# State-space scans of a Mamba block: the inputs dt\*u\*B of five of sixteen states made by TensorE instead of VectorE

## The reference

```python
u, z = jnp.split(xz, 2, axis=-1)             # 256 channels each
u = silu(causal_conv(u) + convb)
dtr, Bm, Cm = jnp.split(u @ Wx.T, [8, 24], axis=-1)   # 16 states
dt = jax.nn.softplus(dtr @ Wdt.T + bdt)
def step(h, ins):                            # over 512 tokens
    dt_t, u_t, B_t, C_t = ins
    h = jnp.exp(dt_t[..., None] * A) * h + (dt_t * u_t)[..., None] * B_t[:, None, :]
    y_t = jnp.einsum('bdn,bn->bd', h, C_t)
    return (h, y_t)
y = (y + u * Dp) * silu(z)                   # then @ Wout.T
```

## Time and profile before

| | us |
|---|---|
| median of three runs | 1843.81 (1840.83 to 1847.52) |
| the profiled execution | 1826.05 |
| span of its instructions | 1824.2 |
| state-space phase in it | about 0 to 1050 |
| mean granted TensorE clock | 0.822 of full |

### The profile page before, as it was taken

The page is one execution under the profiler, slowest core; times in us unless marked ns, Lnnn a source line. Parts: engine busy times, 40 slices in busy tenths (PEclk is TensorE's granted clock), DMA queues, the critical chain, the costliest instruction groups (busy, mean ns, idle before and its releaser), DMA issues. The chain is left out here.

```text
span 1824.2 us, 27919 instructions
## 1 busy us (share of the span) xinstructions
PE 1289.2 (71%) x8048; PEld 890.3 (49%) x8048; DVE 1453.3 (80%) x2426; ACT 953.1 (52%) x1520; POOL 991.7 (54%) x908
## 2 busy tenths in 40 slices
PE   3666767577567667665776627789889898989743
PEld 1444545355445444453554403345666666656643
DVE  1999999999999999999999716577668686767412
ACT  4556646664665466556655122555555555546411
POOL 1677767776777677777777542014244243432443
PEclk9877877787789678877876557989989898999876
DMA  4122302320221122022202021125365454645762
GB/s 144 41 95 94 117 0 93 116 84 9 116 93 76 41 93 116 4 89 116 93 17 93 0 59 52 56 84 172 121 180 176 140 160 137 194 126 169 213 213 58
DMA packets 114407, 184.87 MB, mean 101 GB/s; under 512 B 10385, under 2 KB 87185, under 8 KB 109969
## 3 DMA queue, kind: packets, MB, share of 16 engines
q1 hardware_dynamic: 110192, 175.15, 28.1%
q0 software_dynamic: 4096, 8.40, 1.7%
HBM read 153.03 MB, written 25.89 MB: 98 GB/s over the span
## 5 line engine op out<-in xcount | busy, mean ns | idle before, releaser
L731 POOL TENSOR_TENSOR hc<-hb,cb 128x512 f32<-128x512 f32 x512 | 653.8, 1295 | 249.4 <-DVE hb L610 213.8
L610 DVE TENSOR_TENSOR_SCAN hb<-da,dbu 128x512 f32<-128x512 f32 x512 | 599.4, 1201 | 5.6 <-DVE stats L635 4.0
L499 ACT ACTIVATE da<-dt,a_neg 128x512 f32<-128x512 f32 x512 | 351.9, 717 | 354.6 <-DVE hb L610 303.3
L331 PE MATMUL yp<-ident,hc 128*128 128x128 f32 x2048 | 356.9, 317 | 65.7 <-POOL hc L731 65.4
L331 PEld LDWEIGHTS yp<-ident,hc 128*128 128x128 f32 x2048 | 296.9, 165 | 174.3 <-POOL hc L731 93.6
L603 DVE TENSOR_TENSOR dbu<-dtu,bp 128x512 f32<-128x512 f32 x512 | 323.6, 676 | 3.4 <-PE bp L319 2.5
L1750 DVE TENSOR_REDUCE mx<-ms 128x1 f32<-128x384 f32 (+3 forms) x352 | 219.2, 638 | 128.4 <-PE ms L1333 126.8
L1623 ACT ACTIVATE pt<-scores,lift 128x512 f32<-128x512 f32 x320 | 216.4, 684 | 180.8 <-PE scores L1374 180.2
L319 PE MATMUL bp<-st,sel 96*128 96x512 bf16 x256 | 116.4, 455 | 155.9 <-DVE dbu L603 153.4
L2084 POOL DMA_INDIRECT xs_scratch<-h2n,posi x64 | 63.5, 992 | 164.6 <-issue 115.0
L285 PE MATMUL wp<-xpad,wu 128*128 128x512 f32 x256 | 136.7, 627 | 22.1 <-ACT xpad L429 15.6
(11 more groups left out here) (215 smaller groups left out, 2077.8 us busy)
## 6 DMA issues: line engine op xcount, KB each, us to landing
cb<-c_scratch SPq DMA_DIRECT2D x16, 3072.0 KB, 12.0
wt<-ffn_w_e SPq DMA_DIRECT2D x120, 384.0 KB, 4.2
cb<-c_scratch SPq DMA_DIRECT2D x16, 1024.0 KB, 4.6
q<-q_scratch SPq DMA_DIRECT2D x96, 96.0 KB
xg<-xs_scratch SPq DMA_DIRECT2D x24, 256.0 KB, 4.2
ys_scratch<-ysb SPq DMA_DIRECT2D x24, 256.0 KB, 2.3
q_scratch<-qp SPq DMA_DIRECT2D x24, 128.0 KB
k<-k_scratch SPq DMA_DIRECT2D x32, 72.0 KB
```

Of the source, the lines that this page charges most:

```text
L331: last = nc.tensor.matmul(yp[:, c, h * P:(h + 1) * P], src[:, c * P:(c + 1) * P], ident[:, :], is_transpose=True, start=(s < 0 and h == 0 ...
L499: nc.scalar.activation(da[:, s % NDA, :], dt[:, d, h, :], ACT.Exp, scale=a_neg[:, d, h, n:n + 1]).then_inc(da_done, 1)
L610: nc.vector.tensor_tensor_scan(hb[:, s % NHB, :], da[:, s % NDA, :], dbu[:, s % 2, :], 0.0, ALU.mult, ALU.add).then_inc(scan_done, 1)
L731: nc.gpsimd.tensor_tensor(hc[:, s % NHC, :], hb[:, s % NHB, :], cb[:, d, s // 2, :], ALU.mult).then_inc(hc_done, 1)
```

## The change

Five states, n = 6, 8, 10, 12 and 14, get their input dt\*u\*B from TensorE, in each of the 16 units. TensorE transposes `dtu` (time on partitions, `pe_dtt`, step 3), and ScalarE copies it to SBUF (`dtt`). B with time on partitions comes from small matmuls (`pe_bt`, step 22, for the next unit) and a copy (`bt`). For each such state, ScalarE makes four 128x128 diagonal matrices, the identity scaled by a column of `bt` (`act_diag`), and TensorE multiplies the transposed `dtu` by them (`pe_fill`): 4 f32 matmuls for each half. The first half goes to `bp[n % 2]` at step 2n - 1 in the place of the selection matmul, the second to a bank of `dbu` at step 2n + 2. VectorE's scans read these banks directly. The products of the state behind such a state no longer stand together before its scans: one follows the first scan of the TensorE-made state, the other its second scan. `dt` and `dtu` have one buffer now instead of two.

```diff
+BY_PE = (6, 8, 10, 12, 14)
+def dbu_banks():
+    banks = [0]
+    for n in range(1, NS):
+        banks.append(1 - banks[-1] if made_by_pe(n - 1) else banks[-1])
+    return banks
+def dbu_bank(d, n):
+    return DBU_BANK[n] ^ (d * N_PE % 2)
...
+        def pe_bt(pe, b, d):
+            pe.wait_ge(silu_done, count(silu_done, b, 4 * d + 4))
+            for c in range(TC):
+                for h in range(NH2):
+                    last = nc.tensor.matmul(wp[:, 1 - d, c * NS:(c + 1) * NS], u[:, h, c * P:(c + 1) * P],
+                                            wx[:, d, h, 0:NS], start=(h == 0), stop=(h == 1))
+            last.then_inc(bt_ready, 1)
...
+        def pe_dtt(pe, b, d):
+            pe.wait_ge(dt_done, count(dt_done, b, 2 * d + 2))
+            pe.wait_ge(soft_done, count(soft_done, b, 8 * d + 8))
+            for g in range(2):
+                for c in (2 * g, 2 * g + 1):
+                    for h in range(NH2):
+                        at = (c % 2) * DI + h * P
+                        last = nc.tensor.transpose(wp[:, g, at:at + P], dtu[:, h, c * P:(c + 1) * P], ident[:, :])
+                last.then_inc(dtt_ready, 1)
...
+        def pe_fill(pe, b, d, n, h):
+            e = BY_PE.index(n)
+            if h == 0:
+                pe.wait_ge(diag_done, count(diag_done, b, TC * (N_PE * d + e + 1)))
+                pe.wait_ge(dtt_done, count(dtt_done, b, 2 * d + 2))
+                pe_bank_free(pe, b, d, n)
+            else:
+                pe.wait_ge(scan_done, count(scan_done, b, STEPS * d + 2 * n - 1))
+            dst = dbu[:, dbu_bank(d, n), :] if h else bp[:, n % 2, :]
+            for c in range(TC):
+                last = nc.tensor.matmul(dst[:, c * P:(c + 1) * P], dtt[:, c, h * P:(h + 1) * P], diag[:, e % 2, c, :],
+                                        start=True, stop=True)
+            last.then_inc(fill_done if h else b_ready, 1)
...
@@ pe_dt
             if h == 0:
+                pe.wait_ge(bt_done, count(bt_done, b, d + 1))
...
@@ pe_unit
                 if s % 2 == 1 and s // 2 + 1 < NS:
-                    pe_b(pe, b, d, s // 2 + 1)
+                    if made_by_pe(s // 2 + 1):
+                        pe_fill(pe, b, d, s // 2 + 1, 0)
+                    else:
+                        pe_b(pe, b, d, s // 2 + 1)
+                if s % 2 == 0 and made_by_pe(s // 2 - 1):
+                    pe_fill(pe, b, d, s // 2 - 1, 1)
...
+                if s == 3:
+                    pe_dtt(pe, b, d)
...
+                    if s == 22:
+                        pe_bt(pe, *front)
...
+        def act_diag(act, b, d, e):
+            act.wait_ge(bt_done, count(bt_done, b, d + 1))
+            act.wait_ge(fill_done, count(fill_done, b, N_PE * d + e - 1))
+            for c in range(TC):
+                nc.scalar.activation(diag[:, e % 2, c, :], ident[:, :], ACT.Copy,
+                                     scale=bt[:, d, c, BY_PE[e]:BY_PE[e] + 1]).then_inc(diag_done, 1)
...
@@ act_front
+            if at == 27:
+                act_bt(act, b, d)
@@ act_unit
                 act_da(act, b, d, s)
+                if s in (8, 9):
+                    act_dtt(act, b, d, s - 8)
+                for e in range(N_PE):
+                    if s == 2 * BY_PE[e] - 1:
+                        act_diag(act, b, d, e)
                 if tail and s in (14, 15):
                     act_ygt(act, *tail, s - 14)
...
@@ dve_dbu
             dve.wait_ge(scan_done, count(scan_done, b, STEPS * d + s - 1))
-            nc.vector.tensor_tensor(dbu[:, s % 2, :], dtu[:, d, h, :], bp[:, n % 2, :],
+            nc.vector.tensor_tensor(dbu[:, dbu_bank(d, n) ^ h, :], dtu[:, h, :], bp[:, n % 2, :],
                                     ALU.mult).then_inc(dbu_done, 1)
...
@@ dve_scan
+            n, h = s // 2, s % 2
+            src = dbu[:, dbu_bank(d, n) ^ h, :]
+            if not made_by_pe(n):
+                dve.wait_ge(dbu_done, count(dbu_done, b, N_DBU * d + made_by_dve(s + 1)))
+            elif h == 0:
+                src = bp[:, n % 2, :]
+                dve.wait_ge(b_ready, count(b_ready, b, NS * d + n + 1))
+            else:
+                src = dbu[:, dbu_bank(d, n), :]
+                dve.wait_ge(fill_done, count(fill_done, b, N_PE * d + BY_PE.index(n) + 1))
...
@@ dve_unit
                 dve_scan(dve, b, d, s)
-                if s % 2 == 1 and s + 1 < STEPS:
-                    dve_dbu(dve, b, d, s + 1)
-                    dve_dbu(dve, b, d, s + 2)
+                n, h = s // 2 + 1, s % 2
+                if n < NS and not made_by_pe(n):
+                    if made_by_pe(n - 1):
+                        dve_dbu(dve, b, d, 2 * n + h)
+                    elif h:
+                        dve_dbu(dve, b, d, 2 * n)
+                        dve_dbu(dve, b, d, 2 * n + 1)
```

More of the change, by code:

```diff
@@ L75, in is_first, with made_by_pe, made_by_dve @@
     return isinstance(b, int) and b == 0
+BY_PE = (6, 8, 10, 12, 14)
+N_PE = len(BY_PE)
+def made_by_pe(n):
+    return n in BY_PE
+def made_by_dve(s):
+    return sum(1 for i in range(s) if not made_by_pe(i // NH2))
+N_DBU = made_by_dve(STEPS)
+def dbu_banks():
[3 more added lines that the diff above has]
+    return banks
+DBU_BANK = dbu_banks()
+def dbu_bank(d, n):
+    return DBU_BANK[n] ^ (d * N_PE % 2)
 def mamba_phase(nc, sems, x, x1, cscr, w):
@@ L131, in mamba_phase @@
         t_relu = sb("t_relu", [P, NH2, SEQ])
-        dt = sb("dt", [P, NDIR, NH2, SEQ])
-        dtu = sb("dtu", [P, NDIR, NH2, SEQ])
+        dt = sb("dt", [P, NH2, SEQ])
+        dtu = sb("dtu", [P, NH2, SEQ])
+        dtt = sb("dtt", [P, TC, DI])
+        bt = sb("bt", [P, NDIR, TC, NS])
+        diag = sb("diag", [P, 2, TC, P])
         ud = sb("ud", [P, NH2, SEQ])
@@ L173, in mamba_phase @@
         ygt_ready = sig("ygt_ready", 4, "tensor")
+        fill_done = sig("fill_done", NDIR * N_PE, "tensor")
+        dtt_ready = sig("dtt_ready", 4, "tensor")
+        bt_ready = sig("bt_ready", 2, "tensor")
         out_ready = sig("out_ready", 1, "tensor")
@@ L182, in mamba_phase @@
         ygt_done = sig("ygt_done", 4, "scalar")
+        dtt_done = sig("dtt_done", 4, "scalar")
+        bt_done = sig("bt_done", 2, "scalar")
+        diag_done = sig("diag_done", NDIR * N_PE * TC, "scalar")
         ln_step = sig("ln_step", 16, "vector")
@@ L341, in pe_ygt @@
             elif d:
-                pe.wait_ge(soft_done, count(soft_done, b + 1, 8))
+                pe.wait_ge(dtt_done, count(dtt_done, b + 1, 2))
             else:
-                pe.wait_ge(soft_done, count(soft_done, b, 16))
+                pe.wait_ge(dtt_done, count(dtt_done, b, 4))
             for h in range(NH2):
@@ L408, in _ @@
             pe_xd(pe, 0, 0)
+            pe_bt(pe, 0, 0)
             pe_dt(pe, 0, 0, 0)
@@ L468, in act_xd, with act_bt, act_dtt @@
                 nc.scalar.activation(mid2[:, :], rem[0:32, :], ACT.Copy).then_inc(xd_done, 1)
+        def act_bt(act, b, d):
+            act.wait_ge(bt_ready, count(bt_ready, b, d + 1))
+            act.wait_ge(diag_done, count(diag_done, b, TC * N_PE * (d - 1)))
+            nc.scalar.activation(bt[:, d, :, :], wp[:, 1 - d, 0:TC * NS].rearrange("p (c n) -> p c n", c=TC),
+                                 ACT.Copy).then_inc(bt_done, 1)
+        def act_dtt(act, b, d, g):
+            act.wait_ge(dtt_ready, count(dtt_ready, b, 2 * d + g + 1))
+            act.wait_ge(fill_done, count(fill_done, b, N_PE * d))
+            nc.scalar.activation(dtt[:, 2 * g:2 * g + 2, :], wp[:, g, :].rearrange("p (c n) -> p c n", c=2),
+                                 ACT.Copy).then_inc(dtt_done, 1)
+        def act_diag(act, b, d, e):
[4 more added lines that the diff above has]
+                                     scale=bt[:, d, c, BY_PE[e]:BY_PE[e] + 1]).then_inc(diag_done, 1)
         def act_soft(act, b, d, h, k):
@@ L498, in act_da @@
             act.wait_ge(scan_done, count(scan_done, b, STEPS * d + s + 1 - NDA))
-            nc.scalar.activation(da[:, s % NDA, :], dt[:, d, h, :], ACT.Exp,
+            nc.scalar.activation(da[:, s % NDA, :], dt[:, h, :], ACT.Exp,
                                  scale=a_neg[:, d, h, n:n + 1]).then_inc(da_done, 1)
```

23 lines of the change are left out of this document (15 added, 8 removed).

## The result

| | before | after |
|---|---|---|
| median us | 1845.66 (4 runs, 1840.83 to 1848.10) | 1927.95 (4 runs, 1924.99 to 1933.63) |
| ratio | 1 | 1.0453, 95% interval 1.0417 to 1.0489 |
| span of the profiled execution | 1824.2 | 1928.3 |
| end of the state-space phase in it | 1049.29 | 1125.75 |

The change makes the kernel slower by 82 us; the forecast was +64, between -9 and +96. The end of the phase is the start of the last `x1t` addition on GpSimd. The two phases divide the difference of the spans, 104 us, into 76.5 for the state-space phase and 27.6 for the second phase, which the change doesn't touch; the first experiment deals with the second part.

The account below looks back on a forecast made before the run. VectorE was taken as the state-space phase's clock. Seven plain-and-joint pairs at 9.3 us gave +65, first unit +3, last -4.6, prologue +0.5: +64, so 1908 us from a median of 1843.81; range 1835 to 1940.

Parts of the forecast that it names:

- What bounds: State-space phase: VectorE is the clock, two products and two scans every 3.42 us, waiting 9.0 us in all before them.
- What VectorE gets in return: VectorE's products behind scans of TensorE-made states wait on that scan: 0.13 us each, at most 0.24; 1.3 per unit.
- TensorE's half: Four f32 128x128x128 matmuls per product half: 0.87 us at full clock; ten per unit 8.7 us, less five selection matmuls.
- B's matmuls: TensorE step 22: eight small matmul pairs, 0.5 to 1.7 us, taken as 1.0, hidden under ScalarE's copies.
- Diagonals: ScalarE, 20 per unit: about 0.4 us each, 1.6 for a state's four; bounds 0.16 and 0.5.
- The four places: VectorE scans s13, s17, s21, s25 (numbered s0 to s31), each needing a second half from TensorE's in-order program; delays priced at each.
- plain unit: One of the seven units with d = 1 and front work; forecast +3.1 us, at half clock +4.65.
- my two prices: Plain unit, TensorE from z0 to xd's end: 4.65 us at full clock, 6.2 at half; s21 +4.6 or +6.15.
- Joint unit: One of the seven units with d = 0 that also end a sequence; forecast +4.65 us, at half clock +6.2.
- VectorE as the clock: First rival, faster: TensorE's halves come before VectorE needs them; -74 us, so 1770; decided at n=10's half; chance 0.08.
- the z chain alone: Second rival: only the z chain binds and TensorE's load hides; total -8 us, so 1836; chance 0.09.
- The third: Third rival, dearer: half clock beyond z, diagonals at 0.5, own waits at 0.24; 5 us more per pair, 1943; chance 0.05.

Follow-up runs that it names:

- the first experiment: For the second phase: kernel before, unchanged, profiled again, span 1851.9 us. Under Rivals: changed kernel with selection 11 and n=10's second half ahead of z, 1890.25 us.

## Why the prediction was right, point by point

**What bounds.** Right. VectorE was the clock before, and of the 146 us of waits added at its scans and products 131 end with a half or a selection of TensorE's (87.3 + 46.0 after, 2.5 before).

**What VectorE gets in return.** Right: from s12 (403.45) to the product that waits for it (404.75) it is 1.30 us, from s13 (405.50) to its product (406.75) 1.25. Without such a wait a scan and its successor start 1.12 apart: 0.18 and 0.13 for a wait on itself, against 0.13 taken.

**TensorE's half.** Right: 412.31 to 413.19 is 0.88, against 0.87.

**B's matmuls.** Mis-sized: 16 records in 1.7 us from start to start, the upper bound of my 0.5 to 1.7; I took 1.0, and they don't hide: TensorE has no idle time from the half of n=10 (424.28) to the half of n=12 (431.54).

**Diagonals.** 0.32 each, against 0.4 taken between 0.16 and 0.5: the estimate erred to the dear side, by 0.3 us per batch.

**The four places, plain unit** (later than before, from s0 on):

| | forecast | measured |
|---|---|---|
| s13 | no stall | no stall, -0.2 |
| s17 | +0.8 | +1.0 |
| s21 | +4.6, at half clock +6.15 | +6.2 |
| s21 to the next unit's s0 | -1.5 | -0.5 |
| whole unit | +3.1, at half clock +4.65 | +5.7 |

TensorE waited 1.98 us before z0, and its clock was full for the first z and half for the second: the second of my two prices, for which I had given the middle. The term that failed is the last. s21 to s25 was to take 6.65, with B's matmuls hidden under ScalarE's copies, and took 7.26, as they stand in TensorE's full queue; behind it `dt` took 1.92 us instead of 1.52, which no step of the prediction had.

**Joint unit.** s13 +3.3 (forecast +4.05), s17 +2.9 (+3.5), s21 +6.8 (+6.1 at full, +7.7 at half clock), whole unit +6.6 from s0 to s0, +6.3 by the starts of `dtu`, and +6.1 by these in the mean of the seven (+4.65 or +6.2). The whole comes close to the dear price, but partly by luck: the joint unit's first places were priced 0.6 to 0.8 too dear, and the way from s21 to the next s0 gave back 0.2 where 1.5 was forecast. The waits of the second halves at s13 and s21:
```profile
473.09 1.22 DVE L746 TENSOR_TENSOR_SCAN hb<-da,dbu 128x512 f32<-128x512 f32 x1 [2.55 <-PE dbu L380]
...
493.81 1.22 DVE L746 TENSOR_TENSOR_SCAN hb<-da,dbu 128x512 f32<-128x512 f32 x1 [3.03 <-PE dbu L380]
```

**Sum.** Pair +11.4 (forecast 9.3, between 7.75 and 10.85); first unit +1.35 (+3); last unit -4.9 (-4.6); prologue 0 (+0.5). Together +76.4 against +64, and +82 by the medians. The pair lies above the bounds given for it; the range for the whole held it, as it reached up to +96. Of the 12 us that the sum lacks, 15 are in the pairs, and 2.5 come back in the first unit, the last and the prologue. 11 of the 15 are the clock's: it fell in 12 of the 14 units, and the sum had taken the middle of the two prices.

**Rivals.** VectorE as the clock (-74) and the z chain alone (-8) are both refuted, by the time of the change and by the first experiment: with the half of n=10 ahead of z the kernel still stood 41 us above before, with VectorE waiting for the halves of n=12 in TensorE's queue. The third, dearer by some 5 us per pair, didn't come: the diagonals took 0.32 us where it had 0.5, and VectorE's waits on itself 0.13 to 0.18 where it had 0.24. The point from which the first rival was to decide, the half of n=10, was met there; the rival failed at the next place in the queue.

**What the forecast didn't see.** That there were versions faster than before among the neighbours: states whose halves fall in the slack, and an addition read from another memory.

## What to carry to other kernels

Work moved to an engine with 30% idle time on average is worth what its queue allows at each place: before it, list for each new instruction what stands ahead of it in that engine's program and by when its reader needs it, and after mending one late place look at once at the next one in the queue. Independent work belongs ahead of a wait, where it fills the idle time and, on TensorE, it went with a higher granted clock here. And when an engine is relieved, ask what runs beside it faster or longer than before: here VectorE's relief left GpSimd with a queue of products, and an addition with both inputs in SBUF stood still for them; and it reached the end of its loop before its next instructions were loaded.
